# An attention pass on one NeuronCore: the fourth transposed tile moved behind the next score strips, and scores as three products of fp16 halves

## What is computed

```python
q = (x @ Wq + bq).reshape(B, S, N_HEAD, HEAD_DIM).transpose(0, 2, 1, 3)
k = (x @ Wk + bk).reshape(B, S, N_HEAD, HEAD_DIM).transpose(0, 2, 1, 3)
v = (x @ Wv + bv).reshape(B, S, N_HEAD, HEAD_DIM).transpose(0, 2, 1, 3)
scores = jnp.einsum('bhqd,bhkd->bhqk', q / math.sqrt(HEAD_DIM), k)
scores = scores + attention_bias
scores = jnp.where(src_mask, -jnp.inf, scores.astype(jnp.float32))
probs = jax.nn.softmax(scores, axis=-1).astype(v.dtype)
ctx = jnp.einsum('bhqk,bhkd->bhqd', probs, v)
x = x + (ctx @ Wo + bo)
```

## Time and profile before

| | us |
|---|---|
| median of 3 runs (lowest to highest) | 2863.32 (2859.99 to 2865.2) |
| the profiled execution | 2858.26, its span 2856.0 |
| TensorE busy | 2508.1 (88%) |
| VectorE busy | 2039.3 (71%) |
| GpSimd busy | 1217.7 (43%) |
| ScalarE busy | 1160.5 (41%) |
| one sequence of the attention pass | 152.01 |
| TensorE's granted clock, mean | 0.956 of 2.4 GHz |

### The profile page before, as it was taken

One profiled execution on the slowest core, in us unless ns is written; L12 is line 12 of the kernel. 1 busy time (PEld: TensorE's weight loads), 2 busy tenths in 40 slices (PEclk: granted clock), 3 DMA queues, 4 the chain that ended last, 5 costly groups with the idle time before them and its releaser, 6 DMA issues.

```text
span 2856.0 us, 46535 instructions
## 1 busy us (share of the span) xinstructions
PE 2508.1 (88%) x14115; PEld 1211.6 (42%) x14203; DVE 2039.3 (71%) x3845; ACT 1160.5 (41%) x2197; POOL 1217.7 (43%) x1024
## 2 busy tenths in 40 slices
PE   2788888888888888884999999999999999999991
PEld 1344444444444444442444444444444444444440
DVE  4675756665757666676886878868788687886878
ACT  2465656565555656463232322323223232232321
POOL 3554454535353535452533425334253342433426
PEclk6799999999999999996999999999999999999995
DMA  3444444444444434435322223222232222322222
GB/s 132 136 134 131 148 132 133 132 120 138 126 140 124 138 127 133 132 104 179 129 89 88 89 81 118 89 83 94 81 111 92 85 94 83 111 89 88 92 67 80
DMA packets 155668, 319.38 MB, mean 112 GB/s; under 512 B 17714, under 2 KB 23474, under 8 KB 155458
## 3 DMA queue, kind: packets, MB, share of 16 engines
q1 hardware_dynamic: 145666, 299.13, 32.3%
q10 hardware_dynamic: 9792, 17.83, 1.7%
HBM read 298.85 MB, written 17.86 MB: 111 GB/s over the span
## 4 chain that ended last, share of the span: by engine, by line
PE 39%; issue 7%; DVE 4%; POOL 4%; ACT 1%; DMA 0%; SPq 0%; DVEq 0%; POOLq 0%; ACTq 0%
PE ffn_bank L1328 12%; PE ffn_bank L1330 12%; PE ffn_bank L1329 12%; PE ffn_bank L1321 2%; POOL prod L1249 1%; POOL f L1239 1%; POOL x L1267 1%; PE ffn_bank L1387 1%; PE ffn_bank L1337 0%; ACT g L1449 0%; DVE g2T_hi L1621 0%; DVE tmp L1530 0%; DVE tmp L1570 0%; DMA b<-in_b 0%; DVE g2T_lo L1622 0%
## 5 line engine op out<-in xcount | busy, mean ns | idle before, releaser
L935 DVE CUSTOM_DVE_ANT_0 tiles<-bank,bias 128x512 f32<-128x512 f32 x512 | 323.0, 687 | 221.3 <-PE bank L591 183.4
L751 ACT ACTIVATE tiles<-tiles,nmax 128x512 f32<-128x512 f32 x512 | 363.6, 712 | 249.2 <-DVE nmax L935 249.1
L490 POOL TENSOR_TENSOR bias<-bias,mask_add 128x1024 f32<-128x1024 f32 x128 | 272.0, 2136 | 342.4 <-DMA bias<-in_bias 333.1
L614 PE MATMUL bank<-ident,tiles 128*128 128x128 f32 x2048 | 286.7, 284 | 130.1 <-DVE pT L952 56.8
L614 PEld LDWEIGHTS bank<-ident,tiles 128*128 128x128 f32 x2048 | 223.4, 142 | 206.8 <-ACT tiles L751 80.2
L1621 DVE CAST g2T_hi<-g 128x512 f16<-128x512 f32 x256 | 189.0, 738 | 156.6 <-ACT g L1449 151.7
L1622 DVE TENSOR_TENSOR g2T_lo<-g,g2T_hi 128x512 f16<-128x512 f32 x256 | 270.0, 1055 | 8.8
L1449 ACT ACTIVATE g<-ffn_bank,bi 128x512 f32<-128x512 f32 x128 | 88.0, 687 | 360.4 <-PE ffn_bank L1330 323.0
L1249 POOL TENSOR_TENSOR prod<-grid,f 128x512 f32<-128x512 f32 x108 | 166.6, 1569 | 129.3 <-DMA grid<-in_grids 123.2
L1260 POOL TENSOR_TENSOR prod<-grid,f 128x512 f32<-128x512 f32 x64 | 105.4, 1667 | 265.6 <-DVE tmp L1559 144.7
L1328 PE MATMUL ffn_bank<-w_hi,g2T_hi 128*128 128x512 f16 x512 | 196.1, 383 | 23.8 <-DVE g2T_lo L1622 23.8
(11 more groups left out here) (256 smaller groups left out, 5125.2 us busy)
## 6 DMA issues: line engine op xcount, KB each, us to landing
bias<-in_bias SPq DMA_DIRECT2D x256, 512.0 KB, 4.2
raw<-in_W_l SPq DMA_DIRECT2D x128, 512.0 KB, 3.3
grid<-in_grids SPq DMA_DIRECT2D x172, 256.0 KB, 3.4
xin<-in_x SPq DMA_DIRECT2D x36, 256.0 KB, 4.2
x2n<-x_rows SPq DMA_DIRECT2D x9, 1024.0 KB, 7.1
out<-outt ACTq DMA_DIRECT2D x36, 256.0 KB, 2.0
x_rows<-tiles ACTq DMA_DIRECT2D x32, 256.0 KB, 3.0
l_rows<-in_rows SPq DMA_DIRECT2D x8, 768.0 KB, 4.4
```

The lines of the kernel that those rows point to most:

```text
L490: pool.tensor_tensor(bias[:, n % NB, :, :], bias[:, n % NB, :, :], mask_add[:, u % T, :].unsqueeze(1).to_broadcast([P, 2, S]), ALU.add).th ...
L614: mm = pe.transpose(bank[:, t * P:(t + 1) * P], tiles[:, 4 * (u % NR) + i, t * P:(t + 1) * P], ident[:, :])
L751: act.activation(tile, tile, ACT.Exp, scale=-1.0, bias=nmax[:, u % 2, i:i + 1], accum_out=rsum[:, j, h:h + 1]).then_inc(prob_ready, 1)
L935: dve.tensor_tensor_reduce(tiles[:, 4 * (u % NR) + i, :], bank[:, :], bias[:, half % NB, i % 2, :], -1.0, 3.0e38, ALU.add, ALU.min, nmax[: ...
```

## The change

Scores: q and k are kept as two fp16 halves each instead of one fp32 array. ScalarE writes the high half from the bank; VectorE, once that is there, writes the fp32 value into a scratch array `qk32` and subtracts the high half from it. A strip is then three fp16 products instead of one fp32 product; all four strips' first products go out, then the second ones, then the third. The strips of a group wait for `q_split` and `k_split`, and so does the bank of each projection.

Order: a slot's fourth tile is no longer transposed with the other three but one slot later, right behind the strips of that slot (`turn(u - 2, 3)`). The first two tiles go ahead of the context products, the third behind them. v2 and v3 are projected one slot sooner. R is spread ahead of the first two tiles. On ScalarE the fourth tile is emptied first in the slot, and the banks of `BESIDE` are taken at places given in `ACT_AFTER`; on VectorE they are taken behind the slot's scores, in slots 4 and 5 behind the second of them (`DVE_AFTER`). The definitions of the semaphores are left out here.

```diff
@@ -94,12 +94,13 @@
     return [(v, kb) for v in range(NQ // 2) for kb in range(T) if 2 * v + 3 + kb // 2 == u]
 
 
-BESIDE = {0: [("xT", 0), ("xT", 1)], 1: [("v", 2), ("xT", 2), ("xT", 3)],
-          2: [("v", 3), ("down",), ("q", 1)], 3: [("expert",), ("k", 1)], 4: [("up", 0), ("up", 1)],
-          5: [("up", 2), ("up", 3), ("R", 0)], 6: [("q", 2)], 7: [("k", 2)], 9: [("R", 1)], 10: [("q", 3)],
+BESIDE = {0: [("v", 2), ("xT", 0), ("xT", 1)], 1: [("v", 3), ("xT", 2), ("xT", 3)],
+          2: [("down",), ("q", 1)], 3: [("expert",), ("k", 1)], 4: [("up", 0), ("up", 1)],
+          5: [("R", 0), ("up", 2), ("up", 3)], 6: [("q", 2)], 7: [("k", 2)], 9: [("R", 1)], 10: [("q", 3)],
           11: [("k", 3)], 13: [("R", 2)], 17: [("R", 3)]}
 
-TAKEN_AFTER = {1: 3, 2: 3, 3: 2, 6: 2, 10: 2}
+ACT_AFTER = {0: 3, 1: 3, 3: 2, 5: 0, 6: 3, 7: 3, 9: 0, 10: 3, 11: 3, 13: 0, 17: 0}
+DVE_AFTER = {4: 2, 5: 2}
 ACT_L0 = {9: (("scale0", 0), ("scale0", 1)), 10: (("scale0", 2), ("scale0", 3)),
           14: tuple(("scale1", t) for t in range(T))}
 DVE_L0 = {1: (("expert_weights",),), 6: (("stats0", 0), ("stats0", 1)), 7: (("stats0", 2), ("stats0", 3)),
@@ -116,7 +117,8 @@
         for v, kb in pv_parts(u):
             if v % 2 == 0 and kb == 0:
                 order.append((("ctx", v // 2), 7))
-        keys = BESIDE.get(u, []) + ([("T", u - 1, i) for i in range(4)] if 0 < u <= NQ else [])
+        keys = [("T", u - 2, 3)] if 1 < u <= NQ + 1 else []
+        keys += BESIDE.get(u, []) + ([("T", u - 1, i) for i in range(3)] if 0 < u <= NQ else [])
         for key in keys:
             order.append((key, 4 + ring % 3))
             ring += 1
@@ -166,8 +168,8 @@
         xT = [sb(f"xT_{h}", [P, C, S], F16) for h in ("hi", "lo")]
 
 
-        q32 = sb("q32", [P, C, S], F32)
-        k32 = sb("k32", [P, C, S], F32)
+        q16, k16 = ([sb(f"{n}16_{h}", [P, C, S], F16) for h in ("hi", "lo")] for n in "qk")
+        qk32 = sb("qk32", [P, S], F32)
 
 
         v32 = sb("v32", [P, T, D], F32)
@@ -287,8 +291,8 @@
 
             name, k = key[0], key[-1] if len(key) > 1 else 0
             return {"xT": (xT_split, C, k), "down": (hid_ready, 2, 0), "expert": (hid_ready, 2, 1),
-                    "up": (y_ready, T, k), "x1T": (x1T_split, C, k), "q": (q32_ready, C, k),
-                    "k": (k32_ready, C, k), "v": (v32_ready, T, k), "S": (scored, H * T, k),
+                    "up": (y_ready, T, k), "x1T": (x1T_split, C, k), "q": (q_split, C, k),
+                    "k": (k_split, C, k), "v": (v32_ready, T, k), "S": (scored, H * T, k),
                     "T": (pT_ready[k // 2], H * T // 2, k % 2), "R": (rinv_T_ready, G, k),
                     "ctx": (ctx_ready, G, k), "wo": (x2_ready, T, k)}[name]
 
@@ -580,16 +584,19 @@
                     if u == 0:
                         pe.wait_ge(mask_ready, it * 1 + 1)
                     if j == 0:
-                        pe.wait_ge(q32_ready, it * C + g + 1)
-                        pe.wait_ge(k32_ready, it * C + g + 1)
+                        pe.wait_ge(q_split, it * C + g + 1)
+                        pe.wait_ge(k_split, it * C + g + 1)
                     for i in range(4):
                         bank = claim(pe, it, ("S", u, i))
                         if i >= 2:
                             pe.matmul(bank[:, :], ident_bf[:, :], mask_add[:, j, :], start=True, stop=False)
-                    for i in range(4):
-                        rows = slice(HD * i, HD * i + HD)
-                        pe.matmul(psum[i][:, :], q32[rows, g, j * P:(j + 1) * P], k32[rows, g, :],
-                                  start=i < 2, stop=True).then_inc(full[i], 1)
+                    for part, (w, x) in enumerate(((0, 0), (0, 1), (1, 0))):
+                        for i in range(4):
+                            rows = slice(HD * i, HD * i + HD)
+                            mm = pe.matmul(psum[i][:, :], q16[w][rows, g, j * P:(j + 1) * P], k16[x][rows, g, :],
+                                           start=part == 0 and i < 2, stop=part == 2)
+                            if part == 2:
+                                mm.then_inc(full[i], 1)
 
                 def values(v, kb):
                     g = v // 2
@@ -631,22 +638,25 @@
                 for u in range(SLOTS_ALL):
                     if u < NQ:
                         scores(u)
+                    if 1 < u <= NQ + 1:
+                        turn(u - 2, 3)
                     for key in BESIDE.get(u, []):
                         if key[0] in ("q", "k", "v"):
                             project(key)
-                        elif key[0] != "R":
+                        elif key[0] == "R":
+                            spread(key[1])
+                        else:
                             l0_products(it, key)
+                    if 0 < u <= NQ:
+                        turn(u - 1, 0)
+                        turn(u - 1, 1)
                     if u == NQ + 1:
                         out_products(0)
                         out_products(1)
                     for v, kb in pv_parts(u):
                         values(v, kb)
-                    for g in range(G):
-                        if ("R", g) in BESIDE.get(u, []):
-                            spread(g)
                     if 0 < u <= NQ:
-                        for i in range(4):
-                            turn(u - 1, i)
+                        turn(u - 1, 2)
                 for c in range(C):
                     l0_products(it, ("x1T", c))
                 out_products(2)
@@ -710,10 +720,12 @@
             with act.Fori(0, B) as it:
                 def take(key):
                     name, m = key[0], key[-1]
-                    if name == "q":
+                    if name in ("q", "k"):
+                        hi, scale, b, ready = {"q": (q16[0], 1.0 / (WS * math.sqrt(HD)), bq, q_hi),
+                                               "k": (k16[0], 1.0 / WS, bk, k_hi)}[name]
                         bank = arrived(act, it, key)
-                        act.activation(q32[:, m, :], bank[:, :], ACT.Identity, scale=1.0 / (WS * math.sqrt(HD)),
-                                       bias=bq[:, m:m + 1]).then_inc(q32_ready, 1)
+                        act.activation(hi[:, m, :], bank[:, :], ACT.Identity, scale=scale,
+                                       bias=b[:, m:m + 1]).then_inc(ready, 1)
                     elif name == "v":
                         bank = arrived(act, it, key)
                         act.activation(v32[:, m, :], bank[:, :], ACT.Copy, scale=1.0 / WS).then_inc(v32_ready, 1)
@@ -726,6 +738,7 @@
                         l0_part(it, key)
 
                 take(("q", 0))
+                take(("k", 0))
                 take(("v", 0))
                 take(("v", 1))
 
@@ -740,8 +753,10 @@
                                    bank[:, :].rearrange("p (t q) -> p t q", t=T), ACT.Copy).then_inc(pT_ready[1], 1)
 
                 for u in range(SLOTS_ALL):
+                    if 1 < u <= NQ + 1:
+                        evacuate(u - 2, 3)
                     for i in range(5):
-                        if i == TAKEN_AFTER.get(u, 4):
+                        if i == ACT_AFTER.get(u, 4):
                             for key in BESIDE.get(u, []):
                                 take(key)
                         if i < 4 and u < NQ:
@@ -751,8 +766,7 @@
                             act.activation(tile, tile, ACT.Exp, scale=-1.0, bias=nmax[:, u % 2, i:i + 1],
                                            accum_out=rsum[:, j, h:h + 1]).then_inc(prob_ready, 1)
                     if 0 < u <= NQ:
-                        for i in (2, 3):
-                            evacuate(u - 1, i)
+                        evacuate(u - 1, 2)
                     for part in ACT_L0.get(u, ()):
                         l0_part(it, part)
                     for g in range(G - 1):
@@ -897,10 +911,16 @@
                 dve.tensor_scalar(mask_add[:, :, :], mask_raw[:, :, :], NEG, None, ALU.mult).then_inc(mask_ready, 1)
                 def take(key):
                     name, m = key[0], key[-1]
-                    if name == "k":
+                    if name in ("q", "k"):
+                        hi, lo, scale, b, at_hi, split = {
+                            "q": (*q16, 1.0 / (WS * math.sqrt(HD)), bq, q_hi, q_split),
+                            "k": (*k16, 1.0 / WS, bk, k_hi, k_split)}[name]
                         bank = arrived(dve, it, key)
-                        dve.tensor_scalar(k32[:, m, :], bank[:, :], 1.0 / WS, bk[:, m:m + 1], ALU.mult, ALU.add)\
-                            .then_inc(k32_ready, 1)
+                        dve.wait_ge(at_hi, it * C + m + 1)
+                        if name == "k":
+                            dve.wait_ge(q_split, it * C + m + 1)
+                        link(dve.tensor_scalar(qk32[:, :], bank[:, :], scale, b[:, m:m + 1], ALU.mult, ALU.add))
```

(11 more changed lines are left out.)

8 lines of the change are left out of this document (5 added, 3 removed).

## The result

| | before | after |
|---|---|---|
| median (lowest to highest, 4 runs each) | 2861.65 us (2859.36 to 2865.2) | 2900.99 us (2894.92 to 2905.03) |
| ratio, 95% interval | | 1.0132 (1.0108 to 1.0155) |
| profiled execution, its span | 2858.26, 2856.0 us | 2894.92, 2893.1 us |
| TensorE, VectorE busy in the third sequence | 133.79, 98.06 of 152.01 us | 129.31, 114.23 of 156.96 us |

The change costs 39 us, where I had forecast a gain of 10. On the mean of the seven sequences with a successor it does save TensorE work, 4.0 us a sequence (132.3 to 128.3), and it gives VectorE 13.8 us more (98.4 to 112.3); in the third alone these are 4.5 and 16.

What follows compares the result with a forecast made beforehand. TensorE was nearest its limit, yet idle 18.2 of 152.01 us a sequence; the stretches summed to -2.0 us, with 0.7 added -1.3, times 8 -10.4, from the 2863.3 median to 2853 us, range 2825 to 2885.

Steps and rivals of the forecast that it cites:

- the walk: One sequence of the attention pass priced stretch by stretch, every bank, semaphore and engine order: sum -2.0 us a sequence.
- slots 9 and 10: Waits for the fourth tile and R go in slot 9: 12.8 us instead of 15.99, -3.2.
- slots 13 and 14: Slots at 4.3 and 4.4 us: 8.7 us instead of 14.03, -5.3.
- Strips: Score products: three fp16 sets side by side free TensorE after 0.86 us instead of 1.08.
- B: Clock falls among the transposes of slots 15 and 16: net +0.6 a sequence, 2868 us; chance 0.10.
- Rival C: fp16 strips run one after the other, 2.8 us instead of 0.86: 2980 to 3100 us; chance 0.04.
- Slots 3 to 5: Slot 3 loses 0.6 us, slots 4 and 5 their waits: 21.0 us instead of 23.28, -2.3.
- Slots 4 and 5 lose their waits: In slots 4 and 5 only TensorE's work remains, 5.8 and 6.3 us.
- Rival A: GpSimd stretches the low halves: 2878 us if half are 1.1 us longer, 2909 if all; chance 0.38.
- The argument against it, of time: Outside slots 10 and 11 the subtraction starts at about D + 4.4, GpSimd's addition at about D + 4.9.
- 0.69, always: Profile duration of hT's low half in us, taken as the price of the new splits' subtraction.
- the signs that I had named for being wrong: Subtractions above 1 us, strips above 1.1 us, or a low clock in more places than slot 3.

Runs made afterwards that it cites:

- without the additions: The changed kernel with GpSimd's mask addition cut to 8 of 512 columns, heads 0 and 1 otherwise unmasked: 2814.97 us, 0.984 of the changed kernel.
- load moved: The changed kernel with ScalarE's gelu ahead of slot 2's fourth exponential, moving the exp table load to slot 2: 2876.57 us, against 2900.99.
- the order kernel: New order, q and k in fp32, here with TensorE masking all heads in slots 0 to 5: 2758.6 us; with the gelu early too, 2745.27 us.
- order alone: Against the kernel before, only the new order (fourth tile, v2, v3, each engine's order), q and k kept in fp32: 2780.73 us, ratio 0.9711.
- formed in one step: The changed kernel with low halves as bank minus high half, no scale, bias or fp32 copy: 2817.04 us, 0.9854 of the kernel before.
- the swap of slots 2 and 3: The changed kernel with q(1) projected ahead of the down products in slot 2 and k(1) ahead of the expert's in slot 3: 2894.13 us.

## Why the prediction was wrong

**The base.** I made the walk against the third sequence, 152.01 us. The mean of eight is 150.75: in the third, slots 9 and 10 took 15.99 (14.35 in four of the others) and slots 13 and 14 14.03 (12.68 in four). The granted clock was 0.89 and 0.88 there, and 1.00 in the sequences with 14.35. The third lies 1.3 us above the mean, 10 us in all, and I credited these as gains in every sequence. The other 36 us of the 47 between forecast and profiled change (+36.7 for -10.4) are the 4.5 us, times 8, that after's mean of 155.21 lies above 150.7.

**Strips, rivals B and C.** 0.76 us measured for 0.86 forecast. The Trainium skill ("TensorE: Matmul & The Clock Gate", Part 3) would have given 1.05 by my estimate; the trace is better than both. Rival C is refuted, and B at its place: from slot 15 to the next sequence the clock was 1.00 in five of seven and 0.95 and 0.96 in the others, across the waits among transposes (2.26 and 0.77 us in the third). It was low in slots 0 to 2 (0.81 to 0.89) and in most of slots 3 to 5 (down to 0.84) instead, and besides at 0.92 in slots 6 to 8 of six sequences, which cost nothing (22.26 us with it and without), and at 0.83 in slots 13 and 14 of three (9.81 us, 8.26 in the others).

**The walk.** Slots 0 to 2 +0.3 us against the forecast, slots 6 to 8 -0.4, slots 13 and 14 +0.1: right. Everywhere but in slots 3 to 5 the stretch moved the way that was forecast. **Slots 3 to 5 are the step that failed**: 21.0 forecast, 23.97 measured, +3.0 of the 5.2 us between the forecast's sum and after's. "Slots 4 and 5 lose their waits" held only without the additions (21.17, with the clock at 1.00 in three sequences 20.87). Three things were missing in the term: the low half of hT, held up by GpSimd in seven sequences (1.83 us in the third, where the spread of the reciprocals lost another 1.78); the table load of 1.28, which in the old order was covered in slot 2 and which the walk never moved; and the low clock behind the waits of slots 2 and 3. These three I can't split exactly, since each shortens the others: additions away -2.8 us, load moved -2.5 (with a smaller collision in it). Where no step was held up, on the order kernel, moving the load brought 0.96. The rest of the 5.2 us is smaller: slots 9 and 10 +0.75, slots 11 and 12 +0.7, the end +0.8 (q's low half 1.79 and k's 1.61 us at the loop's start).

**Rival A** had the right mechanism and a size that holds the result (15 to 46 us slower; 39 measured), but mostly at the wrong instructions, so the size is in part luck. It priced only the new low halves. Those lose 0.38 and 0.28 us on the mean (1074 and 968 ns for 690), 21 us of VectorE time in the run. The other operations lose 34 us more than in the kernel before: the low half of the expert's weights 15, hT's low half 13, the spread 8, the rest 2 less. The argument against it, of time (the subtraction ahead of the addition), held where it was made: in slots 2, 3, 6 and 7 one low half of 32 was held up. In slots 10 and 11, where the sum had 0.3 each, they lost 0.46 and 0.57 on the mean; at the loop's start, where the walk had nothing, 1.07 and 0.40. The price came from "0.69, always" for hT's low half; that was a statement about when that operation ran, not about what it is. Of the signs that I had named for being wrong, two came: q's low half above 1 us on the mean, and the clock low in more places than slot 3.

The Trainium skill has the rule for this ("SBUF — State Buffer", Who interferes with whom): a VectorE instruction with two operands in SBUF contends with a GpSimd instruction that reads SBUF, for a pair of ports that only one of them holds at a time. The traces agree: a subtraction that began 0.16 us behind a GpSimd addition of 2.13 took 2.52 us, and the same subtraction with one operand in a bank took 677 to 693 ns, always. The copies and casts that were held up read one operand only; for them the runs alone show it. Had I asked of every such operation in slots 0 to 5 where the additions would fall, a loss would have been the likelier forecast; that is a judgement after the fact, since no run could tell before where they would fall.

**What the split costs.** I priced it at 1.5 us on VectorE and had TensorE's ring of banks wait for it, which is there (48.3 and 41.8 us of waits). But the walk gave only the difference of the two parts, -2.0. By the table, order alone is worth 9.2 us a sequence (150.75 less 141.59), and the halves on top of it cost 13.6 (155.21 less 141.59), of which 10.6 go when the low half is formed in one step.

## What to carry to other kernels

Where two engines compete for a port, an operation's price is its own duration plus a chance to meet the other one, so a change that shifts the time of a chain can cost without touching the operation: look at the maximum of each VectorE step with two on-chip operands and of each copy, and at what GpSimd runs then. A maximum of 0.69 says only that the step did not meet it in this order, and an edit that frees one step can move the collision to the next, as the swap of slots 2 and 3 did. Test the parts of a double change one at a time, since one may pay for the other: here half of the change is a gain of 81 us. Test them together as well, since their prices need not add up. And take a stretch's length from all repetitions of the loop, not from one: the same slots took 14.35 or 15.99 us with the clock.

## What the runs showed of the hardware

- A subtraction of 128x512 numbers with both operands in SBUF took 0.69 to 2.67 us, by what GpSimd did; the same with one operand in a PSUM bank 0.68 to 0.69. Even 128x128 numbers, 0.29 us by themselves, took 2.11.
- A copy and casts of fp32 in SBUF were held up too: 0.43 to 2.21 us, 0.23 to 2.04.
- Four fp16 row strips of 32 rows ran at 0.22 us a set of four, back to back; one product of 128 rows and the same 512 columns takes 0.216 us, so that is the full fourfold.
- GpSimd's mask additions, 16 of 2.13 us a sequence, were worth 39 us in the kernel before and 86 in the changed one. VectorE's idle time for them is not the reason: it idled 32.4 us for them in the whole run before, nearly all ahead of slots 5 and 6, yet slots 3 to 5 gained only 0.3 us a sequence there; and after it idled 3.0. What they hold up beside them on VectorE fits: most of either gain stands in slots 0 to 2.
